# Attention scores from two 64-row strips instead of one 128-row stack with masked key copies

## The chip, the cores and the metric

The kernel runs on one core of one Trainium2 chip. The metric is the device time of one launch in microseconds (us). Three runs of the kernel before gave 665.69, 665.79 and 667.42 us, a median of 665.79 us.

## What is computed

The reference takes x of shape (8, 512, 128), float32, and handles each of the 8 batches alone. The part that the change touches is the attention:

```python
xn = _layernorm(x, axis=-1)                      # B, T, E = 8, 512, 128
q = (xn @ wq).reshape(B, T, H, D)                # H, D = 16, 8
k = ((xn @ w_down) @ wk_up).reshape(B, T, H, D)  # v likewise, with wv_up
q, k = _apply_rope(q, cos, sin), _apply_rope(k, cos, sin)
scores = jnp.einsum('bqhd,bkhd->bhqk', q, k) / sqrt(D)
allowed = pages[None, :] <= pages[:, None]       # pages of 32 tokens
attn = softmax(where(allowed, scores, finfo.min))
s = einsum('bhqk,bkhd->bqhd', attn, v).reshape(B, T, E) @ wo
g = _silu(_L0_ffn_ref(xn, ...))                  # router, top 2 of 8 experts
return x + s * g
```

The second branch is a router with two layers and 8 experts of width 256, all of which are computed for every token and weighted with the two best logits. All results are float32.

## The kernel before, in words

**Batches and stages.** Every engine walks the same written-out list of steps. An opening (`OPENING`) prepares batch 0; then each of the 8 batches goes through `STAGE_B` (router, the 16 half-expert products `layer1`, the 8 products `layer2`, and the row maxima of the scores of head groups 1 to 3) and `STAGE_C` (the scores, their exponentials, and the products with v, `pv`). Some steps belong to the next batch (`AHEAD`): its projections, rotary embedding (`proj`, `split`), the filling of the score operands (`stack`), and the row maxima of its group 0 (`max0`). So TensorE meets the next batch's `max0` between steps 6 and 11 of the current batch's `STAGE_C`. Every engine takes its steps strictly in the list's order, so a wait in one step holds all later steps of that engine.

**The score operands.** The 16 heads form 4 groups of 4. Each q and k is split into a float32r high part and a low part (`roped_hi`, `roped_lo`), and the score is hi*hi + lo*hi + hi*lo. For each group `q_stack` and `k_stack` hold three 32-row slots (4 heads of 8 rows) with these parts, from row 96 on 12 rows that add the causal page mask, and from row 108 on 8 rows that add the negated row maximum. Since a 32-row slot holds all four heads, each head has its own copy of the keys with the other heads' rows set to zero: `k_head[:, 4g+r] = k_stack[:, g] * hmask[:, r]`. VectorE makes the copies of groups 0 and 1 (`heads`, L884), ScalarE those of groups 2 and 3 (`act_head`, L668).

**Filling the stacks.** `stack(b, g)` on the SyncE queue (L385 to L403) issues six transfers within SBUF, of 32 rows each (64 KB), for each group. They wait for `hi_ready` and, for the low parts, `lo_ready`, which VectorE signals at L806 and L808, and for the `pv_done` that frees the operands of the batch before.

**The two uses.** `row_scores` (L515) multiplies a 128-query tile by the keys up to that tile, 256, 384 or 512 columns wide, over rows 0 to 107. VectorE takes the maximum (L856 for group 0, L861 for the others) and negates it (L870, L871); TensorE turns it (L548), ScalarE copies it to `neg_rows` (L658), and SyncE writes it into rows 108 to 115 of `q_stack` (L407). `scores` (L551) then uses all 128 rows with keys stationary and queries moving; ScalarE takes the exponential (L683) and `pv` (L580) uses it. TensorE's score matmuls in `STAGE_C` go to a ring of four PSUM banks, one head in each.

The step lists around the change are:

```python
max_steps = (1, 1, 2, 2, 2, 2, 2, 2, 2, 2, 1, 2, 1, 1, 1, 0)   # per layer1 step
before_pv = {5: [("heads", 0)], 8: [("heads", 1)]}
after_pv = {0: [("proj", 2), ("split", 0), ("proj", 3)], 1: [("split", 1), ("stack", 0)], 4: [("stack", 1)],
            7: [("stack", 2)], 10: [("stack", 3)], NSTEP: [("values", 0), ("negate", 0)]}
```

Of the kernel before, what the change touches and what calls it, by code (L numbers as in the profile page):

```python
# [31 lines left out]
P = 128  # L32
# [6 lines left out]
NG = 4  # L39
# [12 lines left out]
DVE_GROUPS = 2  # L52
NACT = (NG - DVE_GROUPS) * GH
# [5 lines left out]
def stage_b():  # L59
# [10 lines left out]
    for s in range(NL1):  # L70
# [8 lines left out]
        if s < NACT:  # L79
            seq.append(("act_head", s))  # L80
# [6 lines left out]
def stage_c():  # L87

    before_pv = {5: [("heads", 0)], 8: [("heads", 1)]}
# [19 lines left out]
    s for s in STAGE_C if s[0] in ("proj", "split", "stack", "values", "heads", "max0", "negate")]  # L109
# [4 lines left out]
def opening():  # L114
# [5 lines left out]
    seq += [("top", n) for _, n in zip(range(5), top)] + [("heads", 0)]  # L120
    for n in range(NMAX0):
# [3 lines left out]
        if n == 7:  # L125
            seq.append(("heads", 1))
# [28 lines left out]
def build(nc, x, wq, w_down, wk_up, wv_up, wo, rw1, rb1, rw2, rb2, ew1, eb1, ew2, eb2,  # L155
          cos_t, sin_t, ident_c, key_rows, query_rows, head_mask, rank_c, out):
    ctx = ExitStack()
    with ctx:
# [27 lines left out]
        mask_sb = sb("mask_sb", [P, T])  # L186
        hmask = sb("hmask", [P, GH])
# [65 lines left out]
        heads_ready, act_heads_ready = sem("heads_ready"), sem("act_heads_ready")  # L253
# [100 lines left out]
        def _(sp):  # L354
# [65 lines left out]
        def _(pe):  # L420
# [599 lines left out]
```

## Time and profile before

| | |
|---|---|
| median of three runs | 665.79 us |
| span of the profiled execution | 663.7 us |
| PE busy | 607.3 us |
| DVE busy | 467.0 us |
| ACT busy | 354.4 us |

The page gives no total of its own for the profiled execution, only its span from the first to the last instruction; the median of the runs is 2.1 us above that span. PE is TensorE's matmul side and PEld its weight loads, which overlap; DVE is VectorE, ACT is ScalarE, SPq is the SyncE queue that issues the transfers. Since matmuls are pipelined, PE's busy share is no measure of how fast it could go; the distance between the starts of neighbouring matmuls is. Durations in groups of instructions are the mean of one.

### The profile page before, as it was taken

To read this page: it belongs to the slowest core of one execution; us is meant where nothing else is said; L and a number is where in the kernel's file an instruction comes from. 1 tells how busy PE (TensorE), PEld (TensorE's weight loads), DVE (VectorE), ACT (ScalarE), POOL (GpSimd) and SP (SyncE) were. 2 spreads that over 40 slices of the span, in tenths; PEclk is the share of its full clock that TensorE was granted. 3 is DMA by queue.
4 is the path that set the end of the run, shared out by engine and by line. 5 is a ranking of instruction groups with operands and counts; after the bars stand their busy time and mean duration, and the time that the engine had idled before them with its cause. 6 is when DMAs were issued, how large, how long until landed. Compare 5 with 4: busy or idle time off the path is not lost.

```text
span 663.7 us, 12438 instructions
## 1 busy us (share of the span) xinstructions
PE 607.3 (92%) x4116; PEld 448.6 (68%) x4116; DVE 467.0 (70%) x1199; ACT 354.4 (53%) x507; POOL 18.6 (3%) x20
## 2 busy tenths in 40 slices
PE   2569999999999999999999999999999999999895
PEld 1448855787567865678557875788656885578643
DVE  6677866787568866798667865698757875687502
ACT  2123456643766347754576438653576445763573
POOL 0000000000000100001000000001000000000000
PEclk9758999999999989999999999999999998999999
DMA  5810002100120002200021001200021001200000
GB/s 170 210 43 2 3 13 61 27 1 19 38 60 1 18 1 49 46 1 18 21 51 25 1 18 45 50 1 18 1 67 28 2 17 25 51 22 2 19 1 16
DMA packets 21798, 20.93 MB, mean 32 GB/s; under 512 B 4545, under 2 KB 14450, under 8 KB 21778
## 3 DMA queue, kind: packets, MB, share of 16 engines
q1 hardware_dynamic: 21778, 20.67, 12.9%
q8 instruction: 12, 0.20, 0.1%
q14 instruction: 8, 0.07, 0.0%
HBM read 5.45 MB, written 2.10 MB: 11 GB/s over the span
## 4 chain that ended last, share of the span: by engine, by line
PE 70%; DVE 13%; issue 12%; ACT 2%; SPq 1%; DMA 1%; DVEq 0%; POOLq 0%; POOL 0%; ACTq 0%
PE bank L500 15%; PE bank L580 10%; PE ring L517 7%; PE ring L562 7%; PE bank L446 5%; PE bank L447 5%; PE bank L448 5%; PE bank L517 5%; DVE row_max L861 5%; PE ring L565 2%; DVE acc L908 2%; PE ring L566 2%; PE bank L462 1%; ACT probs L683 1%; PE bank L478 1%
## 5 line engine op out<-in xcount | busy, mean ns | idle before, releaser
L683 ACT ACTIVATE probs<-ring 128x768 f32<-128x768 f32 (+1 forms) x192 | 158.9, 880 | 79.7 <-PE ring L562 48.8
L861 DVE TENSOR_REDUCE row_max<-ring 128x2 f32<-128x256 f32 (+1 forms) x192 | 152.3, 819 | 13.1 <-PE ring L517 13.0
L643 ACT ACTIVATE eh<-bank,bias_cols 128x512 f32<-128x512 f32 x128 | 87.8, 686 | 136.9 <-PE bank L448 134.9
L500 PE MATMUL bank<-ew_sb,eh 128*128 128x128 f32 x1024 | 125.8, 276 | 2.4 <-DVE x_lo L786 2.4
L500 PEld LDWEIGHTS bank<-ew_sb,eh 128*128 128x128 f32 x1024 | 120.1, 192 | 5.6 <-issue 3.8
L517 PE MATMUL ring<-k_head,q_stack 108*128 108x256 f32 (+2 forms) x384 | 93.4, 344 | 12.3 <-DVE row_max L861 11.2
L517 PEld LDWEIGHTS ring<-k_head,q_stack 108*128 108x128 f32 x384 | 66.7, 194 | 37.0 <-DVE row_max L861 24.8
L580 PE MATMUL bank<-probs,v_cols 128*32 128x512 f32 (+3 forms) x1024 | 88.0, 442 | 0.4 <-ACT probs L683 0.4
L908 DVE SCALAR_TENSOR_TENSOR acc<-bank,gate_w,acc 128x128 f32<-128x128 f32 x224 | 63.1, 345 | 32.3 <-PE bank L500 32.1
L856 DVE TENSOR_REDUCE row_max<-bank 128x1 f32<-128x128 f32 (+3 forms) x128 | 58.9, 487 | 32.6 <-PE bank L517 31.7
L562 PE MATMUL ring<-q_stack,k_head 128*128 128x512 f32 (+1 forms) x256 | 71.8, 395 | 3.5 <-ACT probs L683 3.5
L562 PEld LDWEIGHTS ring<-q_stack,k_head 128*128 128x128 f32 x256 | 43.1, 193 | 28.5 <-ACT probs L683 19.3
L446 PE MATMUL bank<-x_hi,ew_hi 128*128 128x512 f32 x128 | 59.4, 464 | 2.1 <-DVE bias_cols L749 2.1
L447 PE MATMUL bank<-x_hi,ew_lo 128*128 128x512 f32 x128 | 51.7, 404 | 0.0
L448 PE MATMUL bank<-x_lo,ew_hi 128*128 128x512 f32 x128 | 51.7, 404 | 0.0
L891 DVE COPY o_cols<-bank 128x512 f32<-128x512 f32 x32 | 22.1, 692 | 39.5 <-PE bank L580 39.5
L517 PE MATMUL bank<-k_head,q_stack 108*128 108x256 f32 (+2 forms) x128 | 43.1, 392 | 4.6 <-DVE k_head L884 3.0
L668 ACT ACTIVATE k_head<-k_stack,hmask 128x512 fp32r<-128x512 f32 x64 | 45.4, 712 | 0.0
L517 PEld LDWEIGHTS bank<-k_head,q_stack 108*128 108x128 f32 x128 | 24.6, 202 | 30.4 <-DVE row_max L856 18.5
L580 PEld LDWEIGHTS bank<-probs,v_cols 128*32 128x32 f32 x1024 | 23.4, 108 | 30.0 <-issue 10.5
L884 DVE TENSOR_SCALAR k_head<-k_stack,hmask 128x512 fp32r<-128x512 f32 x64 | 26.7, 482 | 13.5 <-DMA k_stack<-roped_lo 13.5
L565 PEld LDWEIGHTS ring<-q_stack,k_head 128*128 128x128 f32 x128 | 24.1, 188 | 15.1 <-ACT probs L683 15.1
(115 smaller groups left out, 659.4 us busy)
## 6 DMA issues: line engine op xcount, KB each, us to landing
k_stack<-roped_hi SPq DMA_DIRECT2D x64, 64.0 KB, 2.0
q_stack<-roped_hi SPq DMA_DIRECT2D x64, 64.0 KB, 2.0
k_stack<-roped_lo SPq DMA_DIRECT2D x32, 64.0 KB, 2.0
q_stack<-roped_lo SPq DMA_DIRECT2D x32, 64.0 KB, 2.0
out<-out_sb SPq DMA_DIRECT2D x8, 256.0 KB, 2.3
x_all<-in_L_attn_x SPq DMA_DIRECT2D x4, 448.0 KB, 6.9
probs<-in_L_ffn_ew SPq DMA_DIRECT2D x1, 1024.0 KB, 5.8
q_stack<-neg_rows SPq DMA_DIRECT2D x32, 16.0 KB
```

Source lines behind the costliest of these rows:

```text
L446: mm(ps, w_hi, x_hi[:], start=True, stop=False)
L447: mm(ps, w_lo, x_hi[:], start=False, stop=False)
L448: return mm(ps, w_hi, x_lo[:], start=False, stop=True)
L500: last = mm(ps[:, t * E:(t + 1) * E], eh[:, s % EH_RING, t * P:(t + 1) * P], ew2_sb[:, e, f, :], start=(f == 0), stop=(f == HALVES - 1))
L517: return mm(ps[:, 0:width], q_stack[0:MAX0, g, i * P:(i + 1) * P], k_head[0:MAX0, GH * g + r, 0:width], start=True, stop=True)
L562: mm(ring[:, r, j * P:T], k_head[:, h, j * P:(j + 1) * P], q_stack[:, g, j * P:T], start=True, stop=True).then_inc(st_full, 1)
L580: last = mm(wide[g % 2][32 * r:32 * r + 32, dst:T], v_cols[:, tile, GH * g + r, :], probs[:, n % 2, r, src:src + T - dst], start=(tile == ...
L643: nc.scalar.activation(eh[:, s % EH_RING, :], wide[s % 2][:], ACT.Silu, bias=bias_cols[:, s:s + 1]).then_inc(hidden_done, 1)
L683: nc.scalar.activation(probs[:, n % 2, r:r + 2, lo:T], ring[:, r:r + 2, lo:T], ACT.Exp, scale=SCALE).then_inc(exp_done, 1)
L856: V.tensor_reduce(row_max[:, 0, i, r:r + 1], ps[:, 0:(i + 1) * P], AX, ALU.max).then_inc(max0_done, 1)
L861: V.tensor_reduce(row_max[:, g, i, 2 * pair:2 * pair + 2], ring[:, 2 * (m % 2):2 * (m % 2) + 2, 0:(i + 1) * P], AX, ALU.max).then_inc(max_ ...
L908: ins = stt(out=acc[:, t, :], in0=ps[:, t * E:(t + 1) * E], scalar=gate_w[:, t, e:e + 1], in1=(xn if e == 0 else acc)[:, t, :], op0=ALU.mu ...
```

## The change

Each head gets its own operands. A strip is 64 rows, of which 36 or 38 are used: 12 mask rows, then three parts of 8 rows (hi, hi, lo for one side and hi, lo, hi for the other), then 2 rows for the negated maximum. Two neighbouring heads lie in rows 0 to 63 and 64 to 127 of one column block of `q_strip` and `k_strip`, so their matmuls use the two row halves of the TensorE array. The masked copies `k_head`, the steps `heads` and `act_head`, and `hmask` are gone. The strips are not written straight from `roped_hi` and `roped_lo`: the two parts are first stored to device memory (`hi_rows`, `lo_rows`, 512 KB each), SyncE waits until both have landed, and then twelve transfers for each group bring them back, of 8 rows by two heads (32 KB). The negated maxima go by device memory too. All six constant-row transfers into the strips are issued once, before the first `stack`. What TensorE's `max0` and `max_scores` wait for is now all twelve transfers of their group.

```diff
-DVE_GROUPS = 2
-NACT = (NG - DVE_GROUPS) * GH
+NMASK, ONES = MAX0 - MASK0, MAX0 - MASK0
+STRIP = P // 2
+NPART = 3
+STOP0 = NMASK + NPART * D
+ROWS = STOP0 + 2
 NTOP = 11
...
-    before_pv = {5: [("heads", 0)], 8: [("heads", 1)]}
+    before_pv = {}
...
             def stack(b, g, jobs):
-                parts, used = 2 * b + 2, NSTEP * (b - 1) + 3 * g + 2
+                parts, sent, used = 2 * b + 2, 16 * b + 16, NSTEP * (b - 1) + 3 * g + 2
+                if later(b, 1):
+                    sp.wait_ge(pv_done, used)
                 if g == 0:
                     sp.wait_ge(hi_ready, parts)
-                if later(b, 1):
-                    sp.wait_ge(pv_done, used)
-                rows = slice(32 * g, 32 * g + 32)
-                for slot in (0, 1):
-                    sp.dma_start(k_stack[32 * slot:32 * slot + 32, g, :],
-                                 roped_hi[rows, 1, :].bitcast(F32)).then_inc(k_in[g], 16)
-                for slot in (0, 2):
-                    sp.dma_start(q_stack[32 * slot:32 * slot + 32, g, :].bitcast(F32),
-                                 roped_hi[rows, 0, :].bitcast(F32)).then_inc(q_in[g], 16)
-                if g == 0:
+                    sp.dma_start(hi_rows.rearrange("w u s d t -> (u s d) w t"),
+                                 roped_hi[:].bitcast(F32)).then_inc(hi_out, 16)
                     sp.wait_ge(lo_ready, parts)
-                sp.dma_start(k_stack[64:96, g, :], roped_lo[rows, 1, :].bitcast(F32)).then_inc(k_in[g], 16)
-                sp.dma_start(q_stack[32:64, g, :].bitcast(F32),
-                             roped_lo[rows, 0, :].bitcast(F32)).then_inc(q_in[g], 16)
+                    sp.dma_start(lo_rows.rearrange("w u s d t -> (u s d) w t"),
+                                 roped_lo[:].bitcast(F32)).then_inc(lo_out, 16)
+                    sp.wait_ge(hi_out, sent)
+                    sp.wait_ge(lo_out, sent)
+                for strip in (0, 1):
+                    for part in range(NPART):
+                        base = STRIP * strip + NMASK + D * part
+                        k_from, q_from = (hi_rows, lo_rows, hi_rows)[part], (hi_rows, hi_rows, lo_rows)[part]
+                        sp.dma_start(k_strip[base:base + D, 2 * g:2 * g + 2, :].bitcast(F32),
+                                     k_from[1, 2 * g:2 * g + 2, strip].rearrange("u d t -> d u t")).then_inc(k_in[g], 16)
+                        sp.dma_start(q_strip[base:base + D, 2 * g:2 * g + 2, :].bitcast(F32),
+                                     q_from[0, 2 * g:2 * g + 2, strip].rearrange("u d t -> d u t")).then_inc(q_in[g], 16)
             def maxima(b, g, jobs):
-                sp.wait_ge(neg_rows_ready, NG * b + g + 1)
-                sp.dma_start(q_stack[MAX0:MAX0 + MAX_SLOT, g, :].bitcast(F32),
-                             neg_rows[:, g, :]).then_inc(neg_in[g], 16)
+                made, sent = NG * b + g + 1, 16 * (NG * b + g + 1)
+                sp.wait_ge(neg_rows_ready, made)
+                sp.dma_start(max_rows[g].rearrange("p u s t -> (p u s) t"), neg_rows[:, g, :]).then_inc(neg_out, 16)
+                sp.wait_ge(neg_out, sent)
+                for strip in (0, 1):
+                    base = STRIP * strip + STOP0
+                    sp.dma_start(q_strip[base:base + 2, 2 * g:2 * g + 2, :].bitcast(F32),
+                                 max_rows[g, :, :, strip]).then_inc(neg_in[g], 16)
...
             sp.wait_ge(prep_dve, 2)
+            for strip in (0, 1):
+                base = STRIP * strip
+                for tile, w, row, first, n in ((q_strip, 0, base, 0, NMASK), (k_strip, 1, base, 0, NMASK),
+                                               (k_strip, 1, base + STOP0, ONES, 2)):
+                    sp.dma_start(tile[row:row + n].bitcast(F32),
+                                 rows_r[first:first + n, w, :].bitcast(F32).unsqueeze(1).to_broadcast([n, H // 2, T])
+                                 ).then_inc(rows_in_place, 16)
...
             def row_scores(ps, g, i, r):
                 width = max(2, i + 1) * P
-                return mm(ps[:, 0:width], q_stack[0:MAX0, g, i * P:(i + 1) * P], k_head[0:MAX0, GH * g + r, 0:width],
+                u, rows = (GH * g + r) // 2, slice(STRIP * (r % 2), STRIP * (r % 2) + STOP0)
+                return mm(ps[:, 0:width], q_strip[rows, u, i * P:(i + 1) * P], k_strip[rows, u, 0:width],
                           start=True, stop=True)
             def max0(b, n, jobs):
                 i, r = divmod(n, GH)
                 if n == 0:
-                    pe.wait_ge(heads_ready, DVE_GROUPS * b + 1)
-                    pe.wait_ge(q_in[0], 48 * b + 48)
+                    if not later(b, 1):
+                        pe.wait_ge(rows_in_place, 16 * 6)
+                    pe.wait_ge(k_in[0], 16 * 2 * NPART * (b + 1))
+                    pe.wait_ge(q_in[0], 16 * 2 * NPART * (b + 1))
                 ps, full = take(jobs, ("max0", n))
                 row_scores(ps, 0, i, r).then_inc(full, 1)
             def max_scores(b, m, jobs):
                 g, i, pair = 1 + m // NPAIR, m % NPAIR // 2, m % 2
                 if m % NPAIR == 0:
-                    pe.wait_ge(q_in[g], 48 * b + 48)
-                    if g < DVE_GROUPS:
-                        pe.wait_ge(heads_ready, DVE_GROUPS * b + g + 1)
-                if g >= DVE_GROUPS and i == 0:
-                    pe.wait_ge(act_heads_ready, NACT * b + (g - DVE_GROUPS) * GH + 2 * pair + 2)
+                    pe.wait_ge(k_in[g], 16 * 2 * NPART * (b + 1))
+                    pe.wait_ge(q_in[g], 16 * 2 * NPART * (b + 1))
...
             def scores(b, n, jobs):
                 g, j = divmod(n, 3)
                 if j == 0:
-                    pe.wait_ge(neg_in[g], 16 * b + 16)
+                    pe.wait_ge(neg_in[g], 32 * b + 32)
                 if n == 0:
                     pe.wait_ge(max_done, NMAX * b + NMAX)
                 for r in range(GH):
                     if n > 0 and r % 2 == 0:
                         pe.wait_ge(exp_done, NEXP * (NSTEP * b + n - 1) + r // 2 + 1)
-                    h = GH * g + r
+                    u, rows = (GH * g + r) // 2, slice(STRIP * (r % 2), STRIP * (r % 2) + ROWS)
+                    keys, queries = k_strip[rows, u], q_strip[rows, u]
                     if j < 2:
-                        mm(ring[:, r, j * P:T], k_head[:, h, j * P:(j + 1) * P], q_stack[:, g, j * P:T],
+                        mm(ring[:, r, j * P:T], keys[:, j * P:(j + 1) * P], queries[:, j * P:T],
                            start=True, stop=True).then_inc(st_full, 1)
                     else:
-                        mm(ring[:, r, 0:2 * P], k_head[:, h, 3 * P:T], q_stack[:, g, 2 * P:T], start=True, stop=True)
-                        mm(ring[:, r, 2 * P:T], k_head[:, h, 2 * P:3 * P], q_stack[:, g, 2 * P:T],
+                        mm(ring[:, r, 0:2 * P], keys[:, 3 * P:T], queries[:, 2 * P:T], start=True, stop=True)
+                        mm(ring[:, r, 2 * P:T], keys[:, 2 * P:3 * P], queries[:, 2 * P:T],
                            start=True, stop=True).then_inc(st_full, 1)
...
-            def act_head(b, n, jobs):
-
-                g, r = DVE_GROUPS + n // GH, n % GH
-                if r == 0:
-                    act.wait_ge(k_in[g], 48 * b + 48)
-                nc.scalar.activation(k_head[:, GH * g + r, :], k_stack[:, g, :], ACT.Copy,
-                                     scale=hmask[:, r:r + 1]).then_inc(act_heads_ready, 1)
...
-                    for g in range(NG):
-                        dve.wait_ge(q_in[g], 48 * b)
-                        dve.wait_ge(k_in[g], 48 * b)
+                    dve.wait_ge(hi_out, 16 * b)
+                    dve.wait_ge(lo_out, 16 * b)
...
-            def heads(b, g, jobs):
-
-                if isinstance(b, int) and b == 0 and g == 0:
-                    dve.wait_ge(s_const, 16 * (2 + NG))
-                dve.wait_ge(k_in[g], 48 * b + 48)
-                for r in range(GH):
-                    last = ts(k_head[:, GH * g + r, :], k_stack[:, g, :], hmask[:, r:r + 1], None, ALU.mult)
-                last.then_inc(heads_ready, 1)
```

## Rows read from the trace of the kernel before

**Rows 1.** The page: busy time by engine, and the chain that ended last.

```profile
PE 607.3 (92%) x4116; PEld 448.6 (68%) x4116; DVE 467.0 (70%) x1199; ACT 354.4 (53%) x507; POOL 18.6 (3%) x20
...
PE 70%; DVE 13%; issue 12%; ACT 2%; SPq 1%; DMA 1%; DVEq 0%; POOLq 0%; POOL 0%; ACTq 0%
```

**Rows 2.** One router activation per batch: ns min/median/max, then its start.

```profile
L636 ACT ACTIVATE r_act<-bank,bias_cols x1: 690/690/690, 196.7 to 196.7; 128x512 f32<-128x512 f32 x1
...
L636 ACT ACTIVATE r_act<-bank,bias_cols x1: 690/690/690, 274.6 to 274.6; 128x512 f32<-128x512 f32 x1
...
L636 ACT ACTIVATE r_act<-bank,bias_cols x1: 689/689/689, 351.0 to 351.0; 128x512 f32<-128x512 f32 x1
```

**Rows 3.** Timeline (start, us, what, count), STAGE_C step 6 and VectorE before it.

```profile
251.33 0.69 DVE L808 TENSOR_TENSOR roped_lo<-rope_t,roped_hi 128x512 fp32r<-128x512 f32 x1
...
255.90 1.67 DVE L884 TENSOR_SCALAR k_head<-k_stack,hmask 128x512 fp32r<-128x512 f32 x4 [1.92 <-DMA k_stack<-roped_lo]
...
257.47 1.19 PE L562 MATMUL ring<-q_stack,k_head 128*128 128x512 f32 x4
...
258.50 0.40 PE L517 MATMUL bank<-k_head,q_stack 108*128 108x256 f32 x2
```

**Rows 4.** Timeline of the SyncE queue, the same batch.

```profile
251.41 1.17 SPq L394 DMA_DIRECT2D k_stack<-roped_hi  x2
...
254.52 0.59 SPq L402 DMA_DIRECT2D q_stack<-roped_lo  x1
```

**Rows 5.** Transfers: count, KB each, median us from issue to landing.

```profile
k_stack<-roped_lo SPq DMA_DIRECT2D x32, 64.0 KB, 2.0
...
probs<-in_L_ffn_ew SPq DMA_DIRECT2D x1, 1024.0 KB, 5.8
...
sin_sb<-in_sin_t SPq DMA_DIRECT2D x1, 256.0 KB, 3.3
k_stack<-in_key_rows SPq DMA_DIRECT2D x4, 64.0 KB, 2.5
```

**Rows 6.** Timeline of the SyncE queue near the start.

```profile
5.57 1.81 SPq L366 DMA_DIRECT2D k_stack<-in_key_rows  x4
...
23.93 1.25 SPq L394 DMA_DIRECT2D k_stack<-roped_hi  x2
```

**Rows 7.** Chain of waits 240 to 325: start, us that the piece lasted, what.

```profile
254.61 0.99 PE bank L580 x8
...
256.75 0.78 PE bank L580 x8
...
275.50 0.90 PE bank L478 x8
...
287.12 0.48 PE ring L517 x4
...
292.06 0.70 PE ring L517 x4
...
311.62 0.46 PE ring L517 x2
...
319.71 1.05 PE bank L513 x2
```

**Rows 8.** All waits: us in total, times, longest us.

```profile
PEld ring L517 <- DVE row_max L861: 24.8, 48, 1.0
...
DVE q_stack L734 <- DMA hmask<-in_head_mask: 2.0, 1, 2.0
```

**Rows 9.** Stretches: length, busy us (count) by engine, granted clock, DMA share, GB/s.

```profile
20.40:24.90 4.50, 0.04 (x1) 0.00 (x0) 4.33 (x9) 0.00 (x0) 0.00 (x0) 0.99 1.22 290
...
26.00:28.00 2.00, 0.74 (x2) 0.02 (x1) 1.97 (x2) 0.00 (x0) 0.00 (x0) 0.50 0.54 117
...
244.00:246.00 2.00, 2.00 (x6) 1.62 (x5) 0.69 (x1) 0.96 (x2) 0.00 (x0) 0.50 0.00 0
```

**Rows 10.** Timeline of TensorE, the first row-maximum matmul of batch 0.

```profile
36.25 0.79 PE L517 MATMUL bank<-k_head,q_stack 108*128 108x256 f32 x2 [2.99 <-DVE k_head L884]
```

More of the change, by code:

```diff
@@ L78, in stage_b @@
         seq += extra.get(s, [])
-        if s < NACT:
-            seq.append(("act_head", s))
         if s in layer2_at:
@@ L108 @@
 AHEAD = [s for s in STAGE_B if s[0] in ("stats", "norm", "x_cols", "proj")] + [
-    s for s in STAGE_C if s[0] in ("proj", "split", "stack", "values", "heads", "max0", "negate")]
+    s for s in STAGE_C if s[0] in ("proj", "split", "stack", "values", "max0", "negate")]
 MISC = ("router", "logits", "layer2", "out_rows", "out_cols", "project", "weights_t", "neg_max",
@@ L119, in opening @@
     top = iter(range(NTOP))
-    seq += [("top", n) for _, n in zip(range(5), top)] + [("heads", 0)]
+    seq += [("top", n) for _, n in zip(range(5), top)]
     for n in range(NMAX0):
@@ L185, in build @@
         ident = sb("ident", [P, P])
-        mask_sb = sb("mask_sb", [P, T])
-        hmask = sb("hmask", [P, GH])
+        rows_in = sb("rows_in", [P - MASK0, 2, T])
+        rows_r = sb("rows_r", [P - MASK0, 2, T], F32R)
         rank = sb("rank", [P, NE])
@@ L209, in build @@
         roped_lo = sb("roped_lo", [P, 2, T], F32R)
-        q_stack = sb("q_stack", [P, NG, T], F32R)
-        k_stack = sb("k_stack", [P, NG, T])
-        k_head = sb("k_head", [P, H, T], F32R)
+        q_strip = sb("q_strip", [P, H // 2, T], F32R)
+        k_strip = sb("k_strip", [P, H // 2, T], F32R)
+        hi_rows = nc.dram_tensor("hi_rows", (2, H // 2, 2, D, T), F32).ap()
+        lo_rows = nc.dram_tensor("lo_rows", (2, H // 2, 2, D, T), F32).ap()
+        max_rows = nc.dram_tensor("max_rows", (NG, 2, 2, 2, T), F32).ap()
         row_max = sb("row_max", [P, NG, TT, GH])
@@ L252, in build @@
         k_in = [sem(f"k_in{g}") for g in range(NG)]
-        heads_ready, act_heads_ready = sem("heads_ready"), sem("act_heads_ready")
+        hi_out, lo_out, rows_in_place = sem("hi_out"), sem("lo_out"), sem("rows_in_place")
+        neg_out = sem("neg_out")
         max_full, max_done = sem("max_full"), sem("max_done")
@@ L656, in neg_max_t @@
                 if later(b, 1):
-                    act.wait_ge(neg_in[g], 16 * b)
+                    act.wait_ge(neg_in[g], 32 * b)
                 copy(neg_rows[:, g, :], ps[0:MAX_SLOT, :]).then_inc(neg_rows_ready, 1)
@@ L691, in _ @@
                        "weights_t": weights_t, "neg_max": neg_max_t, "gate": gate,
-                      "exp_table": exp_table, "act_head": act_head, "scores": scores, "out_cols": out_cols})
+                      "exp_table": exp_table, "scores": scores, "out_cols": out_cols})
         @block.vector
@@ L730, in constant_rows @@
             def constant_rows():
-                dve.wait_ge(s_const, 16 * (2 + NG))
-                for g in range(NG):
-                    V.tensor_copy(q_stack[MASK0:P, g, :], mask_sb[MASK0:P, :])
+                dve.wait_ge(s_const, 32)
+                V.tensor_copy(rows_r[:], rows_in[:])
                 V.memset(v_cols[:, :, :, D:D + 1], 1.0).then_inc(prep_dve, 1)
@@ L801, in split @@
                 if which == 0 and later(b, 1):
-                    for g in range(NG):
-                        dve.wait_ge(q_in[g], 48 * b)
-                        dve.wait_ge(k_in[g], 48 * b)
+                    dve.wait_ge(hi_out, 16 * b)
+                    dve.wait_ge(lo_out, 16 * b)
                 dve.wait_ge(roped_ready, 2 * b + which + 1)
@@ L935, in _ @@
                   "logits": logits,
-                  "top": top_two, "weights": weights, "max0": max0, "max": max_scores, "negate": negate, "heads": heads, "pv": pv,
+                  "top": top_two, "weights": weights, "max0": max0, "max": max_scores, "negate": negate, "pv": pv,
                   "values": values, "layer2": layer2, "expert_bias": expert_bias,
```

8 lines of the change are left out of this document (2 added, 6 removed).

## Prediction

> **What bounds the kernel now.** I read the page's busy times and chain first. TensorE is busy for 607.3 of 663.7 us and is 70% of the chain that ended last; VectorE, ScalarE and the transfers are far from full [rows 1]. So TensorE, kept in order by its step list, sets the pace, and what counts is how far apart its matmuls start and what makes it wait. Next I took the router's activation, once per batch, as a clock: batches last 77.9 us (196.7 to 274.6) and 76.4 us (274.6 to 351.0) [rows 2]. Then I read the timeline of the batch at 250 us where the next batch's score operands are made. VectorE ends the last split (roped_lo) at 251.33 + 0.69 = 252.02; the masked copies start at 255.90, after a wait for a transfer; TensorE meets the first max0 matmul at 258.50, between scores(6) and pv(5) [rows 3]. So the path from the split to max0 has 258.5 - 251.4 = 7.1 us before TensorE stands still: SyncE issues the first transfer at 251.41 [rows 4]. That slack is what this change spends.
>
> **The path from the split to max0, with the change.** Before: six issues, a landing, four copies, all inside the 7.1 us. After, in order on the SyncE queue: store hi (512 KB), store lo (512 KB), wait for both to land, twelve issues for group 0, and the landing of the last. TensorE waits at max0(0) for all twelve; behind that wait are pv(5) and everything later in its list, and then ScalarE (exponentials) and VectorE, which wait for TensorE.
> - Landing of the stores: the trace shows no store of this size to device memory. The nearest rows are loads: 1024 KB landed 5.8 us after issue, 256 KB 3.3 us after [rows 5]. Lower bound: lo issued at 252.05 and landed 3.3 us later, 255.3. Upper: 251.4 + 0.6 + 5.8 = 257.8. I take 256.4, 5.0 us after the first issue, a little under the 5.8 of the one load of this total size, since that one has further loads queued right behind it in the source.
> - Twelve issues: starts are (254.52 - 251.41) / 5 = 0.62 us apart within a group now [rows 4], and 1.81 / 4 = 0.45 us for loads from device memory at the start of the kernel [rows 6]. The new ones are loads, but with three dimensions; I take 0.55. From first start to last that is 11 x 0.55 = 6.05 us (5.0 to 6.8).
> - Landing of the last: 2.0 us (small transfer inside SBUF) to 2.5 (64 KB load) [rows 5]; I take 2.2.
> - Sum: 256.4 + 0.1 + 6.05 + 2.2 = 264.75, against 258.5: max0 starts 6.25 us late, and with it the rest of the batch. Bounds: 255.3 + 0.1 + 5.0 + 2.0 = 262.4 (3.9 us late) and 257.8 + 0.1 + 6.8 + 2.5 = 267.2 (8.7 late). I take 6.2.
>
> The chain starts at the split, not at TensorE's scores, so whatever TensorE gains in steps 0 to 5 of STAGE_C is swallowed: it arrives at max0 earlier and waits longer. It occurs in 7 batches. The later groups don't wait: SyncE goes on with 12 x 0.55 = 6.6 us for each, so group 1 lands near 271.4, and its first use moves from about 275 to 281; groups 2 and 3 have more room.
>
> The Trainium skill, "DMA: Bandwidth & Descriptors", section "Anatomy of one DMA — SWDGE (gpsimd) path", gives 2.0 us plus bytes / 436 GB/s (for the GpSimd path). By that, as an estimate, 1 MB lands in 4.4 us where I took 5.0, and the sum is 7 x 0.6 = 4 us less; no row here has such a store. The same page advises merging transfers below 64 KB, which this change goes against with 32 KB ones.
>
> **The matmuls.** From the chain, distances between starts: four 256-column row-score matmuls 0.48 (0.12 each), four of 384 0.70 (0.175), two of 512 0.46 (0.23). The logits, with 8 moving columns and 128 stationary ones, still take 0.90 / 8 = 0.112: this is the price of a weight load alone [rows 7]. Two matmuls in the two row halves can stream at once, but the trace has no pair like it. If the two loads go one after the other, a pair lasts 0.11 + its width: 0.34 against 0.46 at 512, 0.285 against 0.35 at 384, nothing at 256. If loads overlap too, a pair lasts as long as one. I take the first, since the 0.112 is the only row that prices a load, and keep the second as the bound.
> - STAGE_C scores: each group has two pairs of 512, two of 384 and the 256s: 2 x 0.12 + 2 x 0.065 = 0.37 us, 1.5 per batch (bound 4 x (2 x 0.23 + 2 x 0.175) = 3.2). Half lies in steps 6 to 11, 0.7; of that I count 0.5, since ScalarE's exponentials share that path (bounds 0 to 1.6).
> - STAGE_B maxima, groups 1 to 3: 6 pairs each of 512 and 384 and 12 of 256 save 1.1 us (bound 6 x 0.23 + 6 x 0.175 + 12 x 0.12 = 3.9).
> - Against it, changing between the full array and halves. The only row with fewer rows is the 32-row bias product: two matmuls of 512 float32 columns last 1.05 [rows 7]; pv steps of float32 tell what such columns cost: eight matmuls, four at a time, last 0.99 at 512 columns and 0.78 at 384 [rows 7], so 0.21 for 2 x 128 columns, 0.42 for 512. Two would be 0.84, so going in and out costs 0.2. STAGE_B has 15 clusters of maxima between layer1 and the rest: 3.0 us. Net +1.9; TensorE waits 24.8 / 8 = 3.1 us per batch for VectorE's maxima there [rows 8] and hides part. I take +1.0 for each of 8 batches (bounds -3.9 and +3.0).
>
> The Trainium skill, "TensorEngine Tiling (Array Packing)", section "Theoretical Speedup", allows up to 2x for contractions of at most 64 rows. By that rule alone the savings would be the bounds of 3.2 and 3.9 us per batch, which is rival D; no row of the trace shows a pair in two row halves.
>
> **The clock.** TensorE idled from 20.4 to 24.9 (0.04 us busy), and at 26 to 28 the granted clock was 0.50, 1.2 GHz; at 244 to 246 it was 0.50 as well [rows 9]. A 6 us wait is longer than the first of these. What it costs: the batch with the slow piece near 244 lasted 77.9 instead of 76.4, 1.5 us. Behind the wait come pv and scores, dense work, so I take 2.0 per batch; bounds 0 and 7, which is all of the 14 us left of STAGE_C at half speed.
>
> **The copies.** The 64 on VectorE and 64 on ScalarE go. Both engines waited for TensorE around them, so I count nothing in the loop. In the last batch STAGE_C has no max0: -0.8.
>
> **The opening.** VectorE no longer waits for the last constant rows, 2.0 us [rows 8], so the first stack issue comes near 21.9 instead of 23.93 [rows 6]. Then: six row transfers 3.3 us, the stores 5.0 plus about 1 for sharing with the x load, strips 8.3: 39.5. max0 was at 36.25 [rows 10], 3.3 us late, less 1.0 for the copies of group 1 that VectorE no longer makes there: +2.3 (bounds 0 and 6).
>
> **Sum.** 7 x (6.2 + 2.0 - 0.5) = 53.9; STAGE_B 8.0; last STAGE_C -0.8; opening +2.3: +63.4 on the 663.7 span, 727.1. Runs are 2.1 above the span: 729.2, say 729.
>
> **Rivals.**
> - A, the transfers at their low ends: 3.9 late instead of 6.2, and the opening 1.0 instead of 2.3. 7 x (3.9 + 2.0 - 0.5) = 37.8, with 8.0 - 0.8 + 1.0: 712. For it: loads at the start take 0.45 to issue. Against: issues in the loop are 0.62 apart. Chance 0.20.
> - B, the clock stays at 1.2 GHz to the end of STAGE_C: 7.0 instead of 2.0, 7 x 5 = 35 more: 764. For it: the half clock after 24.9 is followed by loosely filled TensorE work. Against: the one at 244 was over soon. Chance 0.12.
> - C, the halves don't run side by side, so the change doesn't do what it says: no saving in STAGE_C and the full 3.0 in STAGE_B: 7 x 0.5 + 0.8 + 8 x 2.0 = 20 more: 749. Nothing in the trace excludes it. Chance 0.12.
> - D, faster than before: weight loads of the two halves overlap and switching is free, so each pair costs as one. 7 x (3.9 + 1.0 - 1.6) = 23.1, less 8 x 3.9 = 31.2, less 1.6 in the last STAGE_C, opening 0: -9.7, so 656. It decides once STAGE_B gains more than about 3 us per batch. Against: 0.112 for a load, 1.05 for the bias product, and VectorE's maxima, which would then be late. Chance 0.07. For this one speaks the 2x of the Trainium skill's page "TensorEngine Tiling (Array Packing)", section "Theoretical Speedup"; no run here shows it yet.
>
> The forecast has 0.46, a draw of the terms that ends within 0.3% (about 2 us, what a measurement here can tell from no change) 0.03. Faster 0.07, same 0.03, slower 0.90. The forecast's own range is 705 to 752; with A, B and C it is 698 to 764.
>
> **What would show it.** After: TensorE waits 5 to 8 us for a transfer into a strip before the first max0, seven times, with a granted clock of 0.5 behind it; SyncE issues twelve transfers 0.55 apart after a wait of 4 to 5 us for the stores; batches 84 to 86 us long; L517 pairs of 512 in about 0.34 us. I am wrong if max0 starts without a wait, if the batches are under 80 us, or if the added time lies in STAGE_B.

## The result, and the profile after

The changed kernel takes 766.60 us (median of 4 runs, 759.85 to 766.65) against 666.27 us before, measured beside it: 1.148 times as long [1.145, 1.152]. The forecast of 729 us had the sign right and lies 38 us too low; the measured time is also 2.6 us above the range's upper end of 764. The profiled execution spans 764.7 us, with a mean granted clock of 0.84 against 0.97. Several kernels below have single runs over 1.5% longer than their fastest, at a lower granted clock: their medians take in all runs, their ratios to the kernel before leave these out, and where the profiled execution is one of them, its own time is given.

Busy times and chain of the changed kernel, to be held against [rows 1]:

```profile
PE 651.9 (85%) x4116; PEld 404.1 (53%) x4116; DVE 442.7 (58%) x1132; ACT 314.9 (41%) x443; POOL 18.6 (2%) x20
...
PE 60%; DVE 12%; issue 11%; DMA 8%; SPq 8%; ACT 1%; DVEq 0%; POOLq 0%; POOL 0%; ACTq 0%
```

Transfers and SyncE's queue now hold 16% of the chain (2% before), and TensorE is busy for 44.6 us more with the same 4116 matmuls: they last longer. The router's activation, as in [rows 2], now comes every 89.0 us:

```profile
L652 ACT ACTIVATE r_act<-bank,bias_cols x2: 687/687/687, 326.9 to 415.9; 128x512 f32<-128x512 f32 x2
```

I cut each batch at three starts: the router activation, the first scores matmul (STAGE_C begins) and the first max0 matmul. The first four lines are of the batch that starts at 326.9 us, and at 274.6 before. All times are us; the right column is the forecast's term for the same stretch.

| stretch | before | after | difference | forecast |
|---|---|---|---|---|
| STAGE_B, activation to first scores | 46.9 | 48.0 | +1.1 | +1.0 |
| STAGE_C up to max0 | 13.4 | 18.1 | +4.7 | +6.2 |
| max0 to the next activation | 16.1 | 22.8 | +6.7 | +2.0 - 0.5 |
| one batch | 76.4 | 89.0 | +12.6 | +8.7 |
| activation of batch 1 | 120.3 | 145.2 | +24.9 = 12.6 + 12.3 | 8.7 + 2.3 |
| last STAGE_C and end | 37.8 | 37.2 | -0.6 | -0.8 |

SyncE's queue in the batch at 290 us (start, us, what), the rows that answer to [rows 4]; of the twelve strip transfers the first and the last stand:

```profile
292.79 0.38 SPq L392 DMA_DIRECT2D hi_rows<-roped_hi  x1
293.51 0.37 SPq L395 DMA_DIRECT2D lo_rows<-roped_lo  x1
297.04 0.29 SPq L403 DMA_DIRECT2D k_strip<-hi_rows  x1
...
300.81 0.30 SPq L405 DMA_DIRECT2D q_strip<-lo_rows  x1
```

The stores' landings, against [rows 5], and TensorE's waits, against [rows 8]:

```profile
hi_rows<-roped_hi SPq DMA_DIRECT2D x8, 512.0 KB, 2.8
lo_rows<-roped_lo SPq DMA_DIRECT2D x8, 512.0 KB, 3.5
```

```profile
PE bank L533 <- DMA q_strip<-lo_rows: 49.7, 7, 14.9
...
PE bank L533 <- DMA k_strip<-hi_rows: 5.6, 1, 5.6
```

TensorE waits eight times at max0, 55.3 us in all: 14.9 us in the opening, and 5.0 to 6.2 in each of the seven batches that prepare a next one (in batch 0 it is a transfer from hi_rows that lands last, the 5.6). The chain is the predicted one: store, store, wait, twelve issues, landing, max0. It takes 303.91 - 292.79 = 11.1 us here and 393.05 - 380.90 = 12.15 us in the next batch, where the last transfer took 3.91 us instead of 2.88; I had 13.3. TensorE's timeline around the first of these two waits, and at the end of the second:

```profile
296.31 0.39 PE L581 MATMUL ring<-q_strip,k_strip 38*128 38x256 f32 x2
296.53 0.28 PE L582 MATMUL ring<-q_strip,k_strip 38*128 38x256 f32 x2
296.65 0.28 PE L581 MATMUL ring<-q_strip,k_strip 38*128 38x256 f32 x2
296.77 0.28 PE L582 MATMUL ring<-q_strip,k_strip 38*128 38x256 f32 x2
296.98 0.85 PE L596 MATMUL bank<-probs,v_cols 128*32 128x384 f32 x8
...
303.91 0.68 PE L533 MATMUL bank<-k_strip,q_strip 36*128 36x256 f32 x2 [4.95 <-DMA q_strip<-lo_rows]
```

```profile
393.05 0.68 PE L533 MATMUL bank<-k_strip,q_strip 36*128 36x256 f32 x2 [5.99 <-DMA q_strip<-lo_rows]
```

What follows the wait is the surprise. Stretches of 3 us, with the columns of [rows 9] (behind the busy times of the five engines stands the granted clock):

```profile
297.00:300.00 3.00, 1.76 (x14) 0.50 (x12) 0.00 (x0) 3.00 (x4) 0.00 (x0) 1.00 0.26 66
300.00:303.00 3.00, 0.00 (x0) 0.00 (x0) 0.00 (x0) 0.26 (x1) 0.00 (x0) 0.77 0.41 92
303.00:306.00 3.00, 2.09 (x20) 1.03 (x20) 0.49 (x2) 0.00 (x0) 0.00 (x0) 0.50 0.49 89
...
321.00:324.00 3.00, 3.00 (x20) 1.07 (x21) 1.53 (x3) 2.88 (x4) 0.00 (x0) 0.50 0.03 5
324.00:327.00 3.00, 3.00 (x25) 2.38 (x18) 1.35 (x3) 0.06 (x1) 0.00 (x0) 0.74 0.20 51
327.00:330.00 3.00, 3.00 (x19) 1.98 (x17) 0.91 (x5) 1.58 (x3) 0.00 (x0) 1.00 0.42 80
```

The clock falls to 1.2 GHz in the wait and stays there, although the profile counts TensorE as busy for at least 2.98 us of every stretch of 3 from 306 on. It returns only at the end of STAGE_C, 1.4 us ahead of the next activation: 23.9 us at half clock, and 23.9 to 27.3 in each of the seven batches that have a max0 to wait for.

A long wait is not needed for the fall. The last STAGE_C has no max0, and the longest wait of a TensorE matmul around its start is 1.0 us; yet 6.8 us of it are at half clock, two of them here:

```profile
733.00:735.00 2.00, 2.00 (x16) 0.73 (x14) 0.00 (x0) 1.47 (x2) 0.00 (x0) 0.50 0.00 0
```

The kernel before lost the clock near the start of STAGE_C too, in two of its eight batches, each time for 3.4 us [rows 9].

The opening, against [rows 6] and [rows 10]:

```profile
22.06 0.99 SPq L427 DMA_DIRECT2D q_strip<-rows_r  x1
...
31.40 2.55 SPq L392 DMA_DIRECT2D hi_rows<-roped_hi  x1
...
39.10 0.31 SPq L403 DMA_DIRECT2D k_strip<-hi_rows  x1
```

```profile
46.90 0.58 PE L533 MATMUL bank<-k_strip,q_strip 36*128 36x256 f32 x2 [14.92 <-DMA q_strip<-lo_rows]
```

### The profile page after: what moved, and what is told of

Its sections match the earlier page's. It is cut to its first block, busy times and chain, and to the rows that moved or that the text cites. A ratio compares the mean times of both kernels' runs of the same rounds, so it can differ in the third digit from the quotient of the medians.

```text
span 764.7 us, 12575 instructions
## 1 busy us (share of the span) xinstructions
PE 651.9 (85%) x4116; PEld 404.1 (53%) x4116; DVE 442.7 (58%) x1132; ACT 314.9 (41%) x443; POOL 18.6 (2%) x20
## 3 DMA queue, kind: packets, MB, share of 16 engines
q1 hardware_dynamic: 26694, 30.23, 17.5%
## 4 chain that ended last, share of the span: by engine, by line
PE 60%; DVE 12%; issue 11%; DMA 8%; SPq 8%; ACT 1%; DVEq 0%; POOLq 0%; POOL 0%; ACTq 0%
PE bank L515 13%; PE bank L596 10%; PE bank L533 6%; PE ring L533 6%; PE bank L461 5%; DMA lo_rows<-roped_lo 4%; PE bank L463 4%; PE bank L462 4%; DVE row_max L867 4%; DMA q_strip<-lo_rows 3%; PE ring L578 3%; DVE acc L905 2%; SPq L403 2%; SPq L405 2%; PE bank L477 1%
## 5 line engine op out<-in xcount | busy, mean ns | idle before, releaser
L867 DVE TENSOR_REDUCE row_max<-ring 128x2 f32<-128x256 f32 (+1 forms) x192 | 152.2, 818 | 17.1 <-PE ring L533 16.2
L596 PE MATMUL bank<-probs,v_cols 128*32 128x512 f32 (+3 forms) x1024 | 123.9, 601 | 0.7 <-ACT probs L691 0.7
L533 PE MATMUL bank<-k_strip,q_strip 36*128 36x256 f32 (+2 forms) x128 | 65.5, 623 | 57.3 <-DMA q_strip<-lo_rows 49.7
L533 PEld LDWEIGHTS bank<-k_strip,q_strip 36*128 36x128 f32 x128 | 33.1, 291 | 111.0 <-issue 90.3
L533 PE MATMUL ring<-k_strip,q_strip 36*128 36x256 f32 (+2 forms) x384 | 71.3, 409 | 14.7 <-DVE row_max L867 14.4
L578 PE MATMUL ring<-q_strip,k_strip 38*128 38x512 f32 (+1 forms) x256 | 63.8, 511 | 7.1 <-ACT probs L691 6.4
L533 PEld LDWEIGHTS ring<-k_strip,q_strip 36*128 36x128 f32 x384 | 33.7, 188 | 64.2 <-DVE row_max L867 36.8
L596 PEld LDWEIGHTS bank<-probs,v_cols 128*32 128x32 f32 x1024 | 29.8, 134 | 41.1 <-issue 26.7
L578 PEld LDWEIGHTS ring<-q_strip,k_strip 38*128 38x128 f32 x256 | 30.4, 234 | 36.1 <-ACT probs L691 24.7
L674 ACT COPY neg_rows<-bank 8x512 f32<-8x512 f32 x32 | 18.4, 575 | 30.4 <-PE bank L563 29.5
L581 PE MATMUL ring<-q_strip,k_strip 38*128 38x256 f32 x128 | 30.9, 399 | 0.0
L581 PEld LDWEIGHTS ring<-q_strip,k_strip 38*128 38x128 f32 x128 | 20.8, 246 | 16.7 <-ACT probs L691 16.1
```

The source lines that it names most:

```text
L533: return mm(ps[:, 0:width], q_strip[rows, u, i * P:(i + 1) * P], k_strip[rows, u, 0:width], start=True, stop=True)
L578: mm(ring[:, r, j * P:T], keys[:, j * P:(j + 1) * P], queries[:, j * P:T], start=True, stop=True).then_inc(st_full, 1)
L596: last = mm(wide[g % 2][32 * r:32 * r + 32, dst:T], v_cols[:, tile, GH * g + r, :], probs[:, n % 2, r, src:src + T - dst], start=(tile == ...
L867: V.tensor_reduce(row_max[:, g, i, 2 * pair:2 * pair + 2], ring[:, 2 * (m % 2):2 * (m % 2) + 2, 0:(i + 1) * P], AX, ALU.max).then_inc(max_ ...
```

## Experiments

Theory F ("few rows", called S in the first expectations), formed on the result: the wait starts the half clock, but what keeps it is that the score matmuls cover only 36 or 38 rows per half. Rivals: W, the wait alone does it, and any wait of 5 us costs this much; P, it is the running side by side, which leaves TensorE less filled, that keeps the clock down. Times are medians, ratios are to the kernel before with their 95% interval; "rest" is the stretch from max0 to the next activation. Lines that don't matter are left out of the code.

**before_late**: the kernel before, with three stores, each waited for, ahead of a batch's first stack.

```diff
+if g == 0:
+    for i in range(NLATE):   # 3
+        sp.dma_start(late_rows, roped_hi[0:32, 1, :].bitcast(F32)).then_inc(late, 16)
+        sp.wait_ge(late, 16 * (NLATE * b + i + 1))
```

> The kernel before, with three stores of 64 KB to device memory, each waited for, ahead of each batch's first stack; nothing else is changed. That makes max0 wait some 5 us per batch, as in the changed kernel, but with the old full-array score matmuls. Theory W (the wait alone drops the clock and a STAGE_C at 1.2 GHz is too loosely filled to bring it back): the clock is 0.5 for some 20 to 24 us behind each wait, batches of 86 to 90 us, in all 740 to 765 us. Rival S (the 36-row strip matmuls are what keeps the clock down): the clock is back within about 5 us, batches of 82 to 84 us, in all 710 to 725 us.

706.53 us, 1.062 [1.059, 1.066], a little under the 710 to 725 of rival S. Batches last 82.0: 46.9, 17.5 to max0 (+4.1), rest 17.6 (+1.5). The first max0 matmul of the batch at 291.5 us and the stretches around it:

```profile
355.89 0.57 PE L524 MATMUL bank<-k_head,q_stack 108*128 108x256 f32 x2 [3.97 <-DVE k_head L891]
```

```profile
353.00:357.00 4.00, 1.11 (x10) 0.68 (x14) 2.16 (x6) 0.43 (x1) 0.00 (x0) 0.90 0.43 98
357.00:361.00 4.00, 4.00 (x32) 2.41 (x24) 1.51 (x4) 1.51 (x2) 0.00 (x0) 0.68 0.14 33
361.00:365.00 4.00, 4.00 (x33) 2.73 (x37) 3.21 (x8) 2.60 (x4) 0.00 (x0) 1.00 0.11 25
```

A wait of 4.0 us (4.7 in one batch, with the same outcome) costs the full-array kernel 3.4 us at half clock, and then the clock is back in the midst of STAGE_C. This wait is shorter than the changed kernel's 6; but the strips keep the half clock for 20.5 us behind waits of 2.6 to 2.9 us (hi_first) and of 0.8 to 1.6 us (no_wait, both below), which are shorter still. With these, rival W falls.

**after_filler**: the changed kernel with 20 matmuls of 512 columns ahead of the wait of max0(0).

```diff
+if n == 0:
+    for _ in range(NFILL):   # 20
+        mm(ps[:], w_att_hi[:, 0, :], x_hi[:], start=True, stop=True)
```

> The changed kernel, with twenty 512-column matmuls of projection weights (0.233 us each, 4.7 us) on TensorE ahead of the wait of max0(0), into the bank that max0(0) then overwrites. The strips come no sooner. Theory W: the granted clock stays 1.0, batches of about 82 us, in all 710 to 722 us. Rival S: the clock still falls in STAGE_C, batches near 88 us, in all over 750 us.

731.52 us: one run took 717.43, three 729.63 to 733.81, which is between what the two theories gave. In the profiled execution (733.4) four of six middle batches kept the clock and lasted 81.2 to 81.4: 47.9, 18.1, rest 15.4. The other two lasted 89.8 and 90.1, rest 21.6; both had lost the clock once already around the start of STAGE_C, 21 us before max0. So the undisturbed rest is 15.4, the strips' own gain 16.1 - 15.4 = 0.7, and the price of the clock 22.8 - 15.4 = 7.4 us. That the clock can fall with the wait filled up was not expected.

**hi_first**: the eight transfers that need only hi_rows are issued when that store has landed, the four others after the second.

```diff
-    sp.wait_ge(lo_out, sent)
-for strip in (0, 1): ...
+for low in (False, True):
+    if low and g == 0:
+        sp.wait_ge(lo_out, sent)
+    ...   # the transfers with (source is lo_rows) == low
```

> The changed kernel, with the eight transfers that read hi_rows issued as soon as hi has landed and the four that read lo_rows after them. The last strip of group 0 should land about 2 us sooner, so max0 waits about 3 us instead of 5. Theory W: a shorter wait lets the clock fall less, batches of 78 to 84 us, in all 695 to 725 us. Rival S: only the 2 us are won, 7 x 2 = 14 us, in all about 750 us.

742.76 us, 1.112 [1.105, 1.119]. STAGE_C reaches max0 after 14.9 instead of 18.1; rest 22.6, still with 20.5 us at half clock. Seven times 3.2 is 22 us, about the 24 gained: the queue's time was paid in full, and a wait of 2.8 us instead of 6.0 didn't save the clock.

**rows_same**: the kernel before, maxima of groups 1 to 3 over rows 0 to 63 only, all in the same half.

```diff
-q_stack[0:MAX0, ...], k_head[0:MAX0, ...]
+rows = slice(0, MAX0) if g == 0 else slice(HALF[r % 2], HALF[r % 2] + 64)   # HALF = (0, 0)
+q_stack[rows, ...], k_head[rows, ...]
```

> The kernel before, with the row maxima of groups 1 to 3 taken over rows 0 to 63 of the stacks (the third part and the mask are left out of them). Two neighbouring heads use the same half, so nothing can overlap, and only the switching between the full array and a half is added. If it costs the predicted 0.2 us for each of 15 clusters, partly hidden: 1 to 3 us per batch, in all 674 to 690 us. Rival: switching is free, within 1 us per batch of the kernel before, 662 to 674 us.

694.94 us, 1.045 [1.041, 1.048], slower than expected; STAGE_B 50.5 instead of 46.9, the other stretches as before. 3.6 us over 15 clusters: going into halves and out again costs 0.24 us, and nothing of it is hidden.

**late_rows_same** and **late_rows_apart** (before_late with all score matmuls on 64 rows; both heads of a pair in rows 0 to 63, or in the two halves), and **all_rows_apart** (the latter without the added stores). Each matmul leaves out the part of the score sum that lies in the other half, so these three price TensorE's work and don't compute the attention:

```diff
+HALF = (0, 0)     # late_rows_same; (0, 64) in the other two
+def half(r):
+    return slice(HALF[r % 2], HALF[r % 2] + 64)
 ...   # row_scores and scores take half(r) of q_stack and k_head
```

> before_late, with all score matmuls (maxima and scores) over rows 0 to 63 of the stacks (third part and mask left out), always the same half, so that no two overlap and TensorE is no less occupied than in before_late. Theory F (matmuls on fewer rows of the array don't bring the clock back): 0.5 for 17 us or more behind each wait, in all 765 to 785 us (706.5, 8 x 3.6 for switching, 7 x 5 to 7 for the clock). Rival P (the overlap, which leaves TensorE less filled, is what keeps the clock down): 3.4 us as in before_late, in all about 735 us.

> The same, with neighbouring heads in rows 0 to 63 and 64 to 127, so that they can overlap as in the changed kernel. Both theories F and P: the clock stays at 0.5 for 20 us or more, as in the changed kernel, in all 750 to 765 us. The difference to late_rows_same is the overlap alone: 2.5 us per batch in STAGE_B.

> The kernel before, no transfer added, with all score matmuls over 64 rows in alternate halves (each leaves out a part of the sum). It has the matmuls of the change, the masked copies of before, and no wait. If the matmuls alone gain: STAGE_B 48.0 instead of 46.9, STAGE_C 1 to 2 us shorter, in all 660 to 672 us with the clock at 1.0. If the clock falls without a wait of TensorE: 6 us more in such batches, in all 680 to 715 us.

| | us | ratio | STAGE_B | to max0 | rest | half clock |
|---|---|---|---|---|---|---|
| before_late | 706.53 | 1.062 [1.059, 1.066] | 46.9 | 17.5 | 17.6 | 3.4 |
| late_rows_same | 820.94 | 1.230 [1.227, 1.234] | 50.6-51.0 | 17.9-20.6 | 27.4-27.7 | 27-34 |
| late_rows_apart | 714.12 | 1.072 [1.068, 1.075] | 48.0-48.6 | 17.3-18.2 | 17.1-18.0 | 10 |
| all_rows_apart | 662.75 | 0.995 [0.993, 0.997] | 48.0 | 12.5 | 15.7 | 0 (3.4 in one) |

The batches of late_rows_same are those of an execution of 836.8 us, longer than the median. Two stretches of it, then two of late_rows_apart:

```profile
527.00:531.00 4.00, 4.00 (x30) 1.95 (x29) 1.29 (x2) 3.11 (x4) 0.00 (x0) 0.50 0.00 0
...
800.00:820.00 20.00, 20.00 (x103) 9.73 (x105) 1.38 (x2) 10.96 (x13) 0.00 (x0) 0.50 0.00 0
```

```profile
447.00:451.00 4.00, 4.00 (x29) 2.15 (x33) 2.06 (x6) 1.12 (x2) 0.00 (x0) 0.50 0.22 51
451.00:455.00 4.00, 3.88 (x33) 1.51 (x25) 2.70 (x8) 2.81 (x4) 0.00 (x0) 0.97 0.07 15
```

The two have the same number of rows and the same instructions; only the half differs. With one half used the clock stays at 0.50 to the end of STAGE_C behind a wait of 4.0 us, and in the last STAGE_C (800 to 820), which waits for no transfer at all. With both used the wait is longer, 5.2 us, and the clock is back 4 to 8 us after it. So rival P as put falls: without the running side by side the clock does not come back in 3.4 us, it comes back later. Theory F's numbers missed both: late_rows_same took 821 us, not 765 to 785, having lost the clock in the last STAGE_C and around the start of others as well, and for late_rows_apart F too had expected 20 us or more at half clock and 750 to 765 us, where it was 10 us and 714. What fits both runs is the number of rows in use at one time: a pair in two halves of 64 uses 128, one half 64. That is not all of it: the full array, with 108 to 128 rows, had 3.4 us where the pairs have 10, and whether this comes of the shorter time that pairs take, or of the longer wait, is not shown. all_rows_apart is what pairs gave without late transfers, with the masked copies still made: 0.5%.

**no_wait**: hi_first, with max0 spread over steps 7 to 11 and the six transfers of constant rows ahead of the load of x.

```diff
-at = 6 + n * 6 // NMAX0
+at = 7 + n * 5 // NMAX0
 ...   # and the six constant-row transfers moved up, as in rows_early
```

> hi_first, with the 16 max0 steps spread over steps 7 to 11 of STAGE_C instead of 6 to 11, and the six constant-row transfers issued ahead of the bulk load of x instead of behind it. Theory W (a wait is needed for the clock to fall): no wait, clock 1.0, batches 76 to 78 us, in all 665 to 685 us. Theory F (the strips let it fall without a wait too): half clock in some batches, 690 to 720 us. The opening should be some 8 us shorter than in the changed kernel.

741.64 us, 1.113 [1.109, 1.118]; no faster than hi_first, and outside what either theory gave (at most 720). Waits of 0.8 to 1.6 us were left, so it doesn't do what its name says, and 20.5 us at half clock follow in six batches, 17.1 in the other. Its max0, and two stretches, the second in the last STAGE_C, where no transfer is waited for, the longest wait of a matmul is 0.98 us, for ScalarE, and 13.7 us are at half clock:

```profile
370.64 0.69 PE L537 MATMUL bank<-k_strip,q_strip 36*128 36x256 f32 x2 [1.62 <-DMA q_strip<-lo_rows]
```

```profile
384.00:388.00 4.00, 3.76 (x20) 1.83 (x12) 1.98 (x3) 1.84 (x3) 0.00 (x0) 0.50 0.00 0
...
698.00:702.00 4.00, 4.00 (x24) 1.63 (x20) 0.00 (x0) 1.51 (x2) 0.00 (x0) 0.50 0.00 0
```

**pad64** and **pad64_no_wait**: the changed kernel, and no_wait, with each strip filled to 64 rows (the maxima's negatives at rows 62 and 63, constants between, zero on the query side). The opening has eight more transfers.

```diff
+NEG0 = STRIP - 2
-ROWS = STOP0 + 2
+ROWS = NEG0 + 2
+NPAD = (NEG0 - STOP0) // 2
+for row in (base + STOP0, base + STOP0 + NPAD):
+    sp.dma_start(tile[row:row + NPAD]..., rows_r[NMASK:NMASK + NPAD, w, :]...)
```

> The changed kernel, with each strip filled up to 64 rows: the maxima's rows move to 62 and 63, and the 26 rows between are constants (zero on the query side, so that the scores don't change), put there once by eight more transfers. Every score matmul now covers 62 or 64 rows instead of 36 or 38; instructions, columns and waits are the same. Theory F (the number of rows in use decides whether the clock comes back): 0.5 for some 10 us instead of 24 behind each wait, batches of 82 to 85 us instead of 89, in all 730 to 750 us with an opening that is some 5 to 10 us longer. If rows don't matter: 24 us, batches of 89, in all 770 to 780 us.

> no_wait with the strips filled up to 64 rows in the same way. A wait of about 1.6 us is left. Theory F: the clock stays at 1.0 or dips for under 10 us, batches of 76 to 79 us, in all 680 to 700 us. If rows don't matter: as no_wait, batches of 85, in all over 735 us.

pad64: 745.92 us, 1.120 [1.117, 1.122]. Its batches last 82.9 to 84.2 (48.0, 17.7 to 18.4, rest 16.6 to 18.1), with 6.8 to 10.2 us at half clock, and its first max0 starts at 66.7. The wait is as long as before, or longer:

```profile
474.98 0.69 PE L540 MATMUL bank<-k_strip,q_strip 62*128 62x256 f32 x2 [6.28 <-DMA q_strip<-lo_rows]
```

```profile
473.00:477.00 4.00, 2.02 (x18) 0.99 (x18) 0.49 (x2) 0.00 (x0) 0.00 (x0) 0.50 0.54 68
477.00:481.00 4.00, 4.00 (x23) 1.83 (x21) 1.61 (x4) 1.51 (x2) 0.00 (x0) 0.50 0.16 19
481.00:485.00 4.00, 4.00 (x42) 2.05 (x39) 2.19 (x5) 3.21 (x4) 0.00 (x0) 0.91 0.12 34
```

This is F's clearest case, and it came out as expected: the loop's matmuls, waits and transfers are the changed kernel's, only the row count differs, and the rest falls from 22.8 to 17 or 18. The added rows are zero on the query side, so that what they multiply to is zero: it is the number of rows covered that counts here. pad64_no_wait: 729.93 us, 1.093 [1.087, 1.099], where F had expected 680 to 700; batches from 78.0 (no half clock) to 85.6 (20.5 us of it), with waits of 1.0 to 1.8 us. Full halves alone don't settle it there, and why one batch loses the clock for 20 us and another for none stays open.

**rows_early** and **rows_on_scalar**: the changed kernel with the opening's six constant-row transfers ahead of the load of x, or issued by ScalarE.

```diff
-sp.wait_ge(prep_dve, 2)   # behind the loads: six sp.dma_start(tile[row:row + n]..., rows_r...)
+sp.wait_ge(prep_dve, 2)   # rows_early: the same six, ahead of x_all
+act.wait_ge(prep_dve, 2)  # rows_on_scalar: act.dma_start, in the router step of batch 0
```

> The changed kernel, with the six constant-row transfers issued ahead of the bulk load of x instead of behind it. If they are what made the opening long (they and the first store took SyncE from 22 to 34 us), the first max0 comes at about 39 instead of 46.9 us, in all some 7 us less, 757 to 761 us. If the opening waits for the transfers' own speed, no change, 765 to 768 us.

> The changed kernel with the six constant-row transfers of the opening issued by ScalarE, idle there, instead of by SyncE ahead of the first store. Of the 24.9 us by which the router activation of batch 1 is late, 12.3 belong to the opening. Theory Q, SyncE's queue pays it: the six took 9.3 us to issue (22.06 to 31.40), where 3.3 were predicted, and the store waited behind them. Then the first store is issued near 23 instead of 31.4, the first max0 starts at 38 to 40 instead of 46.9, and the time is 758 to 760. Rival R, the six transfers are slow in themselves (they share the 16 DMA engines with the load of x): wherever they are issued, their data or the stores land as late, the first max0 stays at 45 to 47 and the time at 765 to 767. Should ScalarE's own steps be held up by the issuing, its first router activation starts later than 27.6.

765.35 us, 1.149 [1.142, 1.155], first max0 at 46.1; and 772.56 us, 1.161 [1.152, 1.169] (profiled execution 765.3), first max0 at 47.0. Neither moves the opening by more than 0.8 us, so theory Q (SyncE's queue) falls, and rival R (the six are slow wherever they are issued) is what is left. SyncE's queue in rows_on_scalar shows how:

```profile
10.68 20.98 SPq L380 DMA_DIRECT2D x_all<-in_L_attn_x  x4
31.70 2.36 SPq L383 DMA_DIRECT2D eb_blocks<-in_L_ffn_eb  x4
34.10 0.39 SPq L392 DMA_DIRECT2D hi_rows<-roped_hi  x1
```

Relieved of the six, SyncE now spends 20.98 us on issuing the load of x (8.97 in the changed kernel, 8.94 in the kernel before). In the three orders (the changed kernel, rows_early, rows_on_scalar) the first store is issued at 31.4, 33.1 and 34.1 and lands at 37.8, 36.8 and 37.7. A window of the changed kernel, in which SyncE issues constant rows, moves 73 GB/s at a share of 0.68 (the same window of the kernel before, with its stack transfers: 144 at 0.62). No run leaves the constant rows out, so that R is argued from these times:

```profile
25.00:30.00 5.00, 2.90 (x8) 1.97 (x7) 2.39 (x2) 1.47 (x3) 0.00 (x0) 0.50 0.68 73
```

## Why the prediction was wrong

**The failed step: the price of the clock.** "Behind the wait come pv and scores, dense work, so I take 2.0 per batch; bounds 0 and 7." It is 7.4. The bound was too low as well: 14 us of work at half the clock can take up to 14 us more, not 7. I had priced recovery from a batch of the full-array kernel [rows 2, 9] and called the work behind the wait dense by how many matmuls it holds. before_late shows that this price was about right for that kernel (3.4 us at half clock, 1.5 us lost); late_rows_same, late_rows_apart and pad64 show that it doesn't carry over to matmuls on 36 or 38 rows per half, or on one half alone. Rival B named what happened and gave nearly the right price, 7 of 7.4, but with a chance of 0.12. Seven times 5.4 is 38 us, as much as the whole miss; that nothing else is seen in the total is luck, since the opening (+10.0) and the wait at max0 (-10.5) were off by as much against each other. The Trainium skill, "TensorE: Matmul & The Clock Gate", Part 1, has the gate open again once the engine is busy; here the profile has TensorE busy from 306 to 324, all but 0.02 us, at a granted 0.50, so that the rule as it stands forecasts a return that the trace doesn't show.

**The opening.** Forecast +2.3, measured +12.3, with the first max0 at 46.9 where I had 39.5. The six constant-row transfers took 31.40 - 22.06 = 9.3 us of SyncE where I had 3.3, priced like the strips' loads, though four of them carry 192 KB and the strips' 32; the stores took 7.7 to the first strip transfer (I had 6.0), the strips 7.8 (8.3). That makes max0 10.6 late; the rest comes with batch 0's slower half clock. Rival B's 764 carried the likeliest opening; with that term's upper bound of 6 it would have reached 768, and the range should have ended there. (The forecast's own range, 705 to 752, stands in the prediction without a sum.)

**The wait at max0: right in place, a little too long.** +4.7 for 6.2. SyncE issues every 0.34 us, not 0.55 (11 x 0.21 = 2.3 less), and both stores had landed 4.2 us after the first issue, not 5.0; the last transfer took 2.9 to 3.9, not 2.2. The 4.4 us that the prediction estimated for the two stores from the Trainium skill's fit ("DMA: Bandwidth & Descriptors", section "Anatomy of one DMA — SWDGE (gpsimd) path") was closer to these 4.2 than my reading of the rows, although the fit is given for the GpSimd path and these were issued by SyncE.

**STAGE_B: right by two wrong terms.** +1.1 for +1.0. Switching costs 3.6 (I had 3.0), and running side by side gives back 50.5 - 48.0 = 2.5 (I had 1.1, less what VectorE hides). Weight loads of the two halves do overlap: the timeline above has eight 256-column matmuls in 0.67 us (296.31 to 296.98, where pv begins), with pairs 0.12 apart (296.53, 296.65, 296.77); two loads one after the other would take 2 x 0.112 = 0.224, and the kernel before takes 8 x 0.12 = 0.96 [rows 7]. I had said that nothing is saved at 256. The 0.112 of [rows 7] is the price of loads into the same rows. Rival D's premise on loads was therefore right; what sank it is the switching, which it took as free, the late transfers and the clock.

**Rivals A and C** didn't occur: the +4.7 at max0 lies nearer to A's 3.9 than to my 6.2, but A kept the 2.0 for the clock and a short opening; C's halves that don't overlap are excluded by rows_same against all_rows_apart, STAGE_B of 50.5 against 48.0.

**The sum with measured terms**: 729.2 + 7 x 5.4 + 10.0 - 7 x 1.5 - 7 x 0.2 + 8 x 0.1 + 0.2 = 766.1, against 766.6. What stays open: why a batch of pad64_no_wait or after_filler keeps its clock and the next loses it, and how far the pairing adds to the effect of the rows.

## What to carry to other kernels

Before a matmul is cut down to fewer rows, ask what its neighbours' waits cost at half clock: a gap of 4 us cost the full-array kernel 1.5 us; gaps of 3 to 6 us cost 7 once the work behind them covered 36 to 38 rows per half. A transfer path of many small steps must be added up from the producer to the first use and held against the slack there; its 4.7 us here stand against 0.7 that the pairs gained behind max0. When several terms each have a bound, the far end of the range takes them together.

## What the hardware showed

- Time at 1.2 GHz behind a wait of 4 to 6 us, by the rows that the score matmuls cover: 108 to 128 rows, 3.4 us (before_late); two halves of 62 to 64, 7 to 10 us (pad64, late_rows_apart); two halves of 36 to 38, 24 to 27 us; one half of 64, 24 to 31 us, to the end of the stage (late_rows_same).
- The clock also falls without a long wait: 13.7 us at half clock in no_wait's last STAGE_C, whose longest wait of a matmul is 0.98 us.
- Matmuls in the two row halves overlap with their weight loads: pairs of 256 columns start 0.12 us apart. Leaving the full array for halves and coming back costs 0.24 us (rows_same).
- SyncE issues 32 KB transfers from device memory every 0.34 us (64 KB ones inside SBUF: 0.62, [rows 4]); a 512 KB store to device memory lands 2.8 us after its issue, two in a row 4.2 us after the first issue.
- Constant rows spread over eight column blocks (four transfers of 192 KB, two of 32 KB) took 9.3 us of SyncE; issued by ScalarE, they stretched SyncE's issuing of the load of x from 8.97 to 20.98 us.
